# The queries' turn: a DRAM scratch and a DMA transpose in place of TensorE turns

## What is computed

```python
xn = _layernorm(x, axis=-1)
q = (xn @ Wq.T + bq).reshape(B, S, 32, 32)      # k, v alike
scores = einsum('bshd,bsgd->bshg', q, k) / sqrt(32)
scores = where(scores > 0.001, scores, -inf)
attn = softmax(scores, axis=-1)
ctx = einsum('bshg,bsgd->bshd', attn, v)
x = x + ctx.reshape(B, S, H) @ Wo.T + bo + ffn(xn)   # ffn: int4 gate, up, down weights with scales
```

## Time and profile before

| what | value |
|---|---|
| median of 3 runs | 2102.8 us |
| profiled execution, its own time | 2104.22 us |
| its span in the trace | 2102.2 us |
| mean granted TensorE clock | 0.994 of full speed |
| busy PE / DVE / ACT / POOL | 96 / 76 / 60 / 64 % |
| DMA, mean over the span | 88 GB/s |

### The profile page before, as it was taken

One profiled execution on the slowest core, in us unless ns is written; L12 is line 12 of the kernel. 1 busy time (PEld: TensorE's weight loads), 2 busy tenths in 40 slices (PEclk: granted clock), 3 DMA queues, 4 the chain that ended last, 5 costly groups with the idle time before them and its releaser, 6 DMA issues. The chain is left out here.

```text
span 2102.2 us, 36938 instructions
## 1 busy us (share of the span) xinstructions
PE 2017.6 (96%) x10880; PEld 972.4 (46%) x10880; DVE 1592.0 (76%) x1584; ACT 1252.8 (60%) x2017; POOL 1349.7 (64%) x769
## 2 busy tenths in 40 slices
PE   7899999999998899899999999999999999999997
PEld 5555555555554444334444444444444444444444
DVE  5666766667665300599899989999899989998996
ACT  4578778777775311255666566665656566656653
POOL 1445554645543000058888888888888888888886
PEclk9999999999999999999999999999999999999999
DMA  8363553554454352122122212222112212221208
GB/s 290 91 132 88 106 133 85 113 121 90 111 109 130 101 195 97 30 70 61 45 50 70 60 45 50 53 63 59 48 46 70 60 45 50 68 55 51 50 22 324
DMA packets 330006, 185.97 MB, mean 88 GB/s; under 512 B 269168, under 2 KB 306032, under 8 KB 329968
## 3 DMA queue, kind: packets, MB, share of 16 engines
q1 hardware_dynamic: 329968, 185.46, 34.0%
HBM read 96.29 MB, written 25.17 MB: 58 GB/s over the span
## 5 line engine op out<-in xcount | busy, mean ns | idle before, releaser
L644 PE MATMUL banks<-xt,lower 128*128 128x512 f16 x3584 | 861.7, 379 | 30.0 <-ACT lower L895 16.3
L1212 POOL TENSOR_TENSOR acc<-acc,lower 128x1024 f32<-128x1024 f32 x327 | 772.8, 2368 | 175.2 <-ACT lower L922 175.2
L922 ACT ACTIVATE lower<-banks,down_scale 128x512 f32<-128x512 f32 x654 | 413.8, 683 | 355.9 <-PE banks L669 264.0
L1099 DVE SCALAR_TENSOR_TENSOR lower<-banks,gate_scale,lower 128x1024 f32<-128x1024 f32 x392 | 479.2, 1278 | 146.2 <-PE banks L644 140.2
L644 PEld LDWEIGHTS banks<-xt,lower 128*128 128x128 f16 x3584 | 337.4, 98 | 486.6 <-DVE lower L1099 80.2
L499 PE MATMUL banks<-wt,xt_tile 128*128 128x512 f16 x2304 | 540.0, 380 | 4.2 <-ACT wt L743 2.6
L1099 DVE SCALAR_TENSOR_TENSOR lower<-banks,up_scale,lower 128x1024 f32<-128x1024 f32 x392 | 479.5, 1278 | 51.1 <-PE banks L644 44.9
L669 PE MATMUL banks<-lower 128*128 (+1 forms) x1792 | 458.8, 380 | 5.0 <-DMA lower<-lower 4.4
L1174 POOL TENSOR_TENSOR stacks<-unit,stacks 128x512 f16<-128x512 f32 x192 | 246.7, 1308 | 286.6 <-ACT stacks L768 286.5
L499 PEld LDWEIGHTS banks<-wt,xt_tile 128*128 (+1 forms) x2304 | 215.8, 98 | 220.6 <-issue 4.7
L669 PEld LDWEIGHTS banks<-lower 128*128 (+1 forms) x1792 | 175.2, 98 | 217.6 <-issue 17.3
(11 more groups left out here) (57 smaller groups left out, 1305.8 us busy)
## 6 DMA issues: line engine op xcount, KB each, us to landing
lower<-in_L_ffn_gate_q_dram SPq DMA_DIRECT2D x28, 512.0 KB, 3.7
lower<-in_L_ffn_up_q_dram SPq DMA_DIRECT2D x28, 512.0 KB, 4.5
lower<-in_L_ffn_down_q_dram SPq DMA_DIRECT2D x28, 512.0 KB, 4.1
x_tile<-in_L_attn_x_dram SPq DMA_DIRECT2D x16, 512.0 KB, 3.8
xt_scratch<-xt_tile SPq DMA_DIRECT2D x16, 512.0 KB, 2.8
ctx_scratch<-ctx_parts SPq DMA_DIRECT2D x64, 128.0 KB, 2.1
lower<-ctx_scratch SPq DMA_DIRECT2D x4, 2048.0 KB, 9.2
xt<-xt_scratch SPq DMA_DIRECT2D x4, 2048.0 KB, 15.4
```

The lines of the kernel that those rows point to most:

```text
L644: last = mm(psum[:, 2 * (slot % 3) + c, :], gu_t[:, mat, g, :], xt[:, (2 * half + c) * CT:(2 * half + c + 1) * CT, part, g, :], start=(par ...
L922: run(down_tmp[:, buffer, c * BANK:(c + 1) * BANK], psum[:, 6 + c, :], ACT.Copy, scale=scale)\
L1099: v.scalar_tensor_tensor(out=acc_of[:, half, :], in0=gu_pair(slot % 3), scalar=scale[:, :, :].rearrange("p t k -> p (t k)")[:, bass.ds(t * ...
L1212: g.tensor_tensor(acc[:, half, ho, :], acc[:, half, ho, :], down_tmp[:, buffer, :], ALU.add).then_inc(down_added, 1)
```

## The change

After body i's `store_xt`, SyncE stores the whole queries' stack (1 MB, 8 KB a partition) to a DRAM scratch. It waits for that store to land, and then issues one DMA transpose that reads the scratch as 4096 rows of 128 numbers and writes `turned[:, Q, :]`. The order (token, head slot) of the scratch's rows is the one that the scores want. `turn_k` follows behind. The steps R0 to R3 and their copies are gone, and S0 waits for `q_turned` in place of the copies. In tile 0 the same happens between `turn_x(1)` and `turn_k(0)`.

```diff
+    q_dram = nc.dram_tensor("q_scratch", [P, NH * P], F16).ap()
...
-        STEPS = [["S0"], ["S1"], ["S2"], ["S3"], ["X"], ["T4"], ["T5"], [], ["T6"], [], ["T7"], [], [], ["R0"],
-                 ["R1"], ["R2"], ["R3", "V0"], ["V1"], [], ["V2"], ["V3"], [], [], []]
+        STEPS = [["S0"], ["S1"], ["S2"], ["S3"], ["X"], ["T4"], ["T5"], [], ["T6"], [], ["T7"], [], [], [],
+                 [], [], ["V0"], ["V1"], [], ["V2"], ["V3"], [], [], []]
...
             def scores(j, k):
                 if k == 0:
-                    pe.wait_ge(batch_out[0], j * 4 + 2)
-                    pe.wait_ge(batch_out[1], j * 4 + 2)
+                    pe.wait_ge(q_turned, j * 16 + 16)
                     pe.wait_ge(k_turned, j * 16 + 16)
...
             def first_tile():
                 opening(weights, lambda: None, first_quarter, lambda: None, lambda: None)
-                for m in range(4):
-                    batch(0, m)
...
+            def store_q(i):
+                sp.wait_ge(unit_lo, i * 6 + (2 * Q + 2))
+                anchor(sp)
+
+                wait_pos(sp, q_turned, i * 16)
+                anchor(sp)
+                sp.dma_start(q_dram, stacks[:, Q, :, :].rearrange("p x c -> p (x c)")).then_inc(q_stored, 16)
+
+            def turn_queries(i):
+
+                if isinstance(i, int) and i == 0:
+                    sp.wait_ge(w_turned, 3 * KT)
+                sp.wait_ge(q_stored, i * 16 + 16)
+                anchor(sp)
+                wait_pos(sp, s_done, i * 4)
+                anchor(sp)
+                sp.dma_start_transpose(turned[:, Q, :], q_dram.rearrange("t (x c) -> (t x) c", c=4 * DH))\
+                    .then_inc(q_turned, 16)
...
                     store_xt(i + 1)
                 if projects(i):
+                    store_q(i)
+                    turn_queries(i)
                     turn_k(i)
...
             def first_tile():
                 turn_x(1)
+                store_q(0)
+                turn_queries(0)
                 turn_k(0)
                 store_xt(1)
```

More of the change, by code:

```diff
@@ L165, in build @@
         unit_lo = sem("unit_lo")
+        q_stored = sem("q_stored")
+        q_turned = sem("q_turned")
         k_turned = sem("k_turned")
@@ L270, in steps_of @@
                     if not isinstance(i, int) or i + 1 < TT:
-                        yield kind, n
-                elif kind == "R":
-                    if projects(i):
                         yield kind, n
@@ L341, in build @@
         k_turns = turned[:, K, :].rearrange("p (x t) -> p x t", t=P)
-        def batch_matrix(m):
-            return Q if m < 4 else V
         def batch_dest(eng, j, m):
[L348 to L354, removed]
+            wait_pos(eng, pv_done, j * 4)
+            return turned[:, V, :].rearrange("p (t x) -> p t x", x=NH)\
                 [:, :, 8 * (m % 4):8 * (m % 4) + 8]
@@ L505, in batch @@
             def batch(j, m):
-                mat = batch_matrix(m)
                 if m % 4 == 0:
-                    pe.wait_ge(unit_lo, j * 6 + (2 * mat + 2))
-                wait_pos(pe, batch_out[m % 2], j * 4 + m // 2)
+                    pe.wait_ge(unit_lo, j * 6 + (2 * V + 2))
+                wait_pos(pe, batch_out[m % 2], j * 2 + (m // 2 - 2))
                 for n in range(8):
-                    last = turn(batch_bank(m)[:, n * P:(n + 1) * P], stacks[:, mat, 8 * (m % 4) + n, :], ident16[:])
+                    last = turn(batch_bank(m)[:, n * P:(n + 1) * P], stacks[:, V, 8 * (m % 4) + n, :], ident16[:])
                 last.then_inc(batch_done, 1)
@@ L535, in head_products @@
                 if k == 0:
-                    pe.wait_ge(batch_out[0], j * 4 + 4)
-                    pe.wait_ge(batch_out[1], j * 4 + 4)
+                    pe.wait_ge(batch_out[0], j * 2 + 2)
+                    pe.wait_ge(batch_out[1], j * 2 + 2)
                     pe.wait_ge(s_out, j * 4 + 4)
@@ L601, in tile_2 @@
                     for kind, n in steps_of(i, s):
-                        if kind == "R":
-                            batch(i, n)
-                        elif kind == "T":
+                        if kind == "T":
                             batch(i - 1, n)
@@ L760, in unit_part @@
                 act.wait_ge(unit_copied, i * 6 + (u + 1))
[L762 to L765, removed]
+                if u // 2 == V:
+                    wait_pos(act, batch_done, i * 4)
+                else:
+                    wait_pos(act, q_stored if u // 2 == Q else k_turned, i * 16)
                 dst, src = stack_view(u, HI), unit_view(u)
@@ L771, in batch_copy @@
             def batch_copy(j, m):
-                act.wait_ge(batch_done, j * 8 + (m + 1))
+                act.wait_ge(batch_done, j * 4 + (m - 3))
                 dst = batch_dest(act, j, m)
@@ L834, in tile_2 @@
                             x_part(i + 1)
-                        elif kind == "R" and n % 2 == 0:
-                            batch_copy(i, n)
                         elif kind == "T" and n % 2 == 0:
@@ L863, in first_tile @@
                 opening(weights, lambda: x_part(0), first_quarter, lambda: root(1), lambda: x_part(1))
-                batch_copy(0, 0)
-                batch_copy(0, 2)
             walk(act, first_tile, tile_2)
@@ L996, in batch_copy @@
             def batch_copy(j, m):
-                dve.wait_ge(batch_done, j * 8 + (m + 1))
+                dve.wait_ge(batch_done, j * 4 + (m - 3))
                 dst = batch_dest(dve, j, m)
@@ L1046, in tile_2 @@
                             x_part(i + 1)
-                        elif kind == "R" and n % 2:
-                            batch_copy(i, n)
                         elif kind == "T" and n % 2:
@@ L1081, in first_tile @@
                 opening(weights, lambda: x_part(0), first_quarter, next_norm, lambda: x_part(1))
-                batch_copy(0, 1)
-                batch_copy(0, 3)
             walk(dve, first_tile, tile_2)
```

## The result

The changed kernel takes 2218.64 us (median of 5 runs, 2217.32 to 2221.1); the kernel before 2102.8 us in the same comparison. The ratio is 1.0554, with a 95% interval of 1.0539 to 1.0568: slower by 116 us. The profiled execution took 2218.94 us, its span 2217.1 us. The forecast was 2230 us.

What follows compares the result with a forecast made beforehand. TensorE's order of work was taken to set the 38.94 us period; the change would make SyncE's queue late. Tile 0's 3.1, 116.2 for 14 bodies and body 15's 7.6 sum to 127 us: 2230 us, range 2175 to 2315.

Steps and rivals of the forecast that it cites:

- sign of 7 us or more: Before each S0, a TensorE gap of 7 us or more, released by the DMA into `turned`, would show the forecast right.
- What is removed: On TensorE, four batches of turns and a 0.54 us wait go: 2.3 us a tile, if S0's operands are there.
- Step 1: SyncE's queue in a steady body: the x store's issue ends 28.5 us after S0, a chain the change leaves as is.
- Step 2: The 1 MB queries' store to DRAM: 4.8 us after a 0.2 us gap, landing 33.5 us after S0.
- Step 3: The queries' turn from DRAM takes K's price, 4.8 us, from 33.7 to 38.5 us after S0.
- the second rival's plain rate: The queries' turn from DRAM runs as a plain load, 2.9 instead of 4.8 us: 2200 us; chance 20%.
- Step 4: K's turn, queued behind, is issued at 38.7 and lands 6.7 us later; S0 at 45.6, 6.7 us more a tile.
- Step 5: TensorE's clock falls after each stall before S0, slowing S0 to S3: 1.6 us more a tile.
- The ends: Outside bodies 1 to 14: tile 0 adds 3.1 us and body 15 adds 7.6 us with the clock.
- The slower turn from DRAM: The queries' turn from DRAM runs slower than K's: at twice the price 2307 us; chance 15%.
- The clock that doesn't matter: Stall too short, or slow S0 to S3 hidden behind ScalarE's copies: 24 us less, 2206 us; chance 12%.
- The new link that fits the gap: The new work fits into SyncE's gap and TensorE sets the period again: about 2083 us; chance 4%.

Runs made afterwards that it cites:

- K's turn first: Changed kernel with K's turn issued ahead of the queries' turn, behind the queries' store, in tile 0 too; 2193.0 us, ratio 1.0432.
- early store: Changed kernel with the queries' store issued ahead of the four turns of the probabilities; 2135.9 us, ratio 1.0157.
- TensorE kept busy: Changed kernel with 28 matmuls of unused result put on TensorE just ahead of S0's wait in bodies 1 to 15; 2189.8 us, ratio 1.0417.
- turns back: Changed kernel with TensorE's four batches of turns of the queries put back, their results left unread; 2220.65 us, ratio 1.0564.
- the last run: Against the run with the late x store, tile 0's queries' store also goes ahead of its x turn; 2105.6 us, ratio 1.0017.
- the run with the late x store: Against the run with the early store, the x store is put behind K's turn; 2112.2 us, ratio 1.0042.
- the run with the turn from SBUF: Changed kernel with the queries turned straight from SBUF, no DRAM store or wait, scores of mixed queries; 2160.3 us, ratio 1.0268.

## Why the prediction was right

**The mechanism** held in each step: SyncE's queue in series, K's turn late behind the store, the wait and the queries' turn; TensorE's removed work swallowed; the clock down after every stall. The period was to be about 47 us and is 46.56; the stall before S0 was to be 7 to 8 us and is 6.4 to 6.8 in all bodies but one (7.2), so its sign of 7 us or more was missed by a little. The queries' turn, 1 us shorter than forecast, accounts for that. Four of the runs took one link each by itself: the wait (K's turn first), the store with its wait (early store), the clock (TensorE kept busy) and TensorE's own work (turns back).

**What is removed** (2.3 us a tile, counted only if S0's operands are there): worth nothing, by the run with the turns put back. V0 waits about 1.1 us for the probabilities, as said, and that too is swallowed.

**Step 1**, 28.5 us from S0 to the end of the x store's issue: in the body shown it is 391.26 - 360.07 = 31.2, which is 28.5 and 2.7 of clock. **Step 2**, store with its gap, 5.0 us: 5.11 (the landing 4.6 for 4.8; the gap ahead of it 0.36 for 0.2). **Step 3**, the queries' turn with its gap, 5.0 us: 4.03. This is the term that was mis-sized most. K's price was taken for it, and a DRAM source is about 1 us cheaper (3.78 us of SyncE's time). It lies midway between K's price and the second rival's plain rate of 2.9 us. The prediction named a queries' turn of another length than K's as a sign of being wrong in this step, and that sign came. **Step 4**, from K's issue to S0, 6.9 us: 6.92. **Step 5**, the clock, 1.6 us: 2.1 by the filled stall. The term was taken from a stretch of the opening with about 3 us at half clock. Here the half clock lasted from 3 to 6 us after S0, and nothing hides it: S3 comes 6.5 to 8.2 us after S0 where it came 5.24 after it before, and in bodies 2 to 14 the probabilities' turns go out 23.4 to 25.0 us after S0, where in the run with the filled stall it is 22.1. Together 8.3 us forecast and 7.67 measured; over the 14 bodies 116 and 107. The turn was 1.0 us too dear and the clock 0.5 too cheap, so half of the one error was made up by the other, which is luck.

**The ends**: tile 0 was to add 3.1 us (its own terms give 3.0) and adds 1.8, the queries' turn again 1 us shorter (3.76). Body 15 was to add 7.6 and adds 6.4. The shift goes through, but not by the context load alone. TensorE now stands 7.59 us at 778.44 for the load of Wo, which lies behind K's turn in the queue as well, and only 0.84 us for the contexts at 785.58, where it stood 2.30 for them before. The prediction named the contexts only.

**The rules.** The Trainium skill, Advanced Engine Details and Errata, X-Bar Transpose, has a transposing DMA as fast as a plain one. Here a megabyte takes 3.8 us from DRAM and 4.8 from SBUF, both of SyncE's time, where the plain rate of the earlier trace rows gives 2.9. So it holds for neither source here, for DRAM better than for SBUF. The Trainium skill, VectorE: DVE Perf Modes, The three transpose paths, gives 1309 ns for a block turned by DMA. Here it is 3.78 us / 32 = 0.12 us a block when 32 are turned in one issue, so the page's figure can't be used for such an issue.

**The rivals.** The plain rate: the direction was right, its size half. The slower turn from DRAM: excluded. The clock that doesn't matter: excluded, 29 us hang on it. The new link that fits the gap: it doesn't in the changed order. The prediction had K's turn go out by 344.5, 32.1 us after S0, for TensorE to set the period. In bodies 2 to 14 of the last run it goes out 31.9 to 32.5 us after S0, and the period is 38.9 to 39.6 us, so that point is about right. The 2083 us of the rival, though, didn't come: the freed time is idle, as said. The 1.1 us a tile that it counted are 1.2 by its own rows (339.23 - 338.03).

## What to carry to other kernels

A DMA that waits for another DMA on an in-order queue charges that DMA's whole latency, here 4.6 us, to everything behind it. Before such a pair is added, ask which transfer behind it is awaited last, and put the first of the pair where the queue idles anyway: here that alone was worth 83 of 116 us. And work taken off the busiest engine is worth nothing if what feeds it becomes late, as the 1.8 us a tile here. The stall is then paid twice, once in idle time (6.5 us) and once in the clock after it (2.1 us).

## What was not expected of the hardware

A 1 MB transpose from DRAM held SyncE for 3.8 us and one from SBUF for 4.8; right behind the x store it was 4.6 and 5.5. The one from DRAM varies: with no store right ahead of it, in the run with the late x store, it took about 4.0 us in most bodies and up to 4.6. A plain 1 MB store beside a transpose from SBUF stretched the transpose from 4.8 to 6.2 us (7.3 in tile 0).

TensorE's clock didn't follow from the length of the idle spell alone. In the run with the early store one spell of 2.48 us ended at half clock and the next, of 2.55, at full:

```profile
326.50 0.97 PE L519 MATMUL banks<-turned 128*128 128x128 f16 x8 [2.48 <-DMA turned<-stacks]
...
368.58 0.62 PE L519 MATMUL banks<-turned 128*128 128x128 f16 x8 [2.55 <-DMA turned<-stacks]
```

In the run with the turn from SBUF a spell of 3.41 us ended at full clock, and the fall to half came only after S0, in the matmuls behind it:

```profile
378.56 0.62 PE L519 MATMUL banks<-turned 128*128 128x128 f16 x8 [3.41 <-DMA turned<-stacks]
379.01 2.09 PE L491 MATMUL banks<-wt,xt_tile 128*128 128x512 f16 x6
380.89 1.06 PE L519 MATMUL banks<-turned 128*128 128x128 f16 x8
```

Spells of 1.0 to 1.8 us (the last two runs, steady bodies) were followed by full speed: the granted clock is 1.00 in every window of 40 us from 155 to 595. At 2.15 us one was followed by a fall behind the first eight matmuls (the run before the last, S0 at 122.54) and at 2.16 us one was not (the last run, tile 0). What decides between 2.1 and 3.4 us these runs don't settle.
